# Softplus as one ScalarE function, five of sixteen B products on GpSimd, loops written out: a linear-attention and selective-scan kernel

## The reference

```python
xz = x @ W_in
xh, z = jnp.split(xz, 2, axis=-1)
xh = jax.nn.silu(_causal_conv_k2(xh, conv_w, conv_b))
x_dbl = xh @ W_x
dt_low = x_dbl[..., :DT_RANK]
Bmat = x_dbl[..., DT_RANK:DT_RANK + D_STATE]
Cmat = x_dbl[..., DT_RANK + D_STATE:]
dt = jax.nn.softplus(dt_low @ W_dt + b_dt)
A = -jnp.exp(A_log)
# for every pixel t:  h = exp(dt_t*A)*h + dt_t*B_t*x_t ;  y_t = sum over the states of h*C_t
y = _selective_scan(xh, dt, Bmat, Cmat, A, D)      # + xc * D
y = y * jax.nn.silu(z)
return y @ W_out
```

## Time and profile before

| what | value |
|---|---|
| median of 3 runs | 17306.35 us (17305.44 to 17314.31) |
| the profiled execution's own time | 17308.57 us |
| its span, first to last instruction | 17306.8 us, 188395 instructions |
| PE | 14501.2 us busy (84%) |
| DVE | 14618.9 us busy (84%) |
| ACT | 10286.0 us busy (59%) |
| POOL | 13647.4 us busy (79%) |
| mean granted TensorE clock | 0.886 |

### The profile page before, as it was taken

One profiled execution on the slowest core, in us unless ns is written; L12 is line 12 of the kernel. 1 busy time (PEld: TensorE's weight loads), 2 busy tenths in 40 slices (PEclk: granted clock), 3 DMA queues, 4 the chain that ended last, 5 costly groups with the idle time before them and its releaser, 6 DMA issues. The chain is left out here.

```text
span 17306.8 us, 188395 instructions
## 1 busy us (share of the span) xinstructions
PE 14501.2 (84%) x40250; PEld 5566.1 (32%) x40250; DVE 14618.9 (84%) x14056; ACT 10286.0 (59%) x14202; POOL 13647.4 (79%) x5903
## 2 busy tenths in 40 slices
PE   8999978888888888888888888888888888888876
PEld 3444433333333333333333333333333333333322
DVE  1222239999999999999999999999999999999942
ACT  2222236666666666666666666666666666666642
POOL 0000019999999999999999999999999999999930
PEclk9999988888888888888888888888888888888865
DMA  1111114444444444444444444444444444444445
GB/s 52 38 41 40 43 42 159 159 160 161 161 162 160 157 159 159 160 162 160 162 160 160 156 159 160 162 160 162 160 160 156 159 160 162 160 162 160 160 186 209
DMA packets 508191, 2499.22 MB, mean 144 GB/s; under 512 B 53097, under 2 KB 164938, under 8 KB 226651
## 3 DMA queue, kind: packets, MB, share of 16 engines
q1 hardware_dynamic: 489723, 2419.71, 37.7%
q10 hardware_dynamic: 18208, 76.11, 1.2%
HBM read 2325.05 MB, written 170.57 MB: 144 GB/s over the span
## 5 line engine op out<-in xcount | busy, mean ns | idle before, releaser
L734 POOL TENSOR_TENSOR hc<-h,c_all 128x1024 f32<-128x1024 f32 x4096 | 9526.1, 2354 | 287.9 <-PE y_ps L975 283.2
L975 PE MATMUL y_ps<-hc,ident 128*128 128x512 f32 x16392 | 8032.1, 635 | 900.2 <-POOL hc L734 899.5
L850 ACT ACTIVATE d_a<-dt,a_neg 128x512 f32<-128x512 f32 x8194 | 5596.4, 688 | 4243.9 <-DVE h L1079 4195.4
L1079 DVE TENSOR_TENSOR_SCAN h<-d_a,h,dbx_v 128x512 f32<-128x512 f32 x4960 | 6087.2, 1264 | 25.1
L975 PEld LDWEIGHTS y_ps<-hc,ident 128*128 128x128 f32 x16392 | 3185.3, 203 | 5870.4 <-issue 3862.9
L723 POOL TENSOR_TENSOR dbx_p<-dtx,b_all 128x1024 f32<-128x1024 f32 x1536 | 3613.9, 2353 | 168.4 <-DVE h L1079 168.1
L1079 DVE TENSOR_TENSOR_SCAN h<-d_a,h,dbx_p 128x512 f32<-128x512 f32 x2976 | 3654.0, 1262 | 42.2 <-ACT d_a L850 36.3
L1066 DVE TENSOR_TENSOR dbx_v<-dtx_ps,b_all 128x1024 f32<-128x1024 f32 x2560 | 3013.3, 1201 | 12.9 <-issue 9.3
L479 POOL MEMSET ident_f<- 128x128 f32 x1 | 0.2, 204 | 2438.4 <-POOLq L44 2438.4
L272 PE MATMUL conv_ps<-image,w_taps 128*32 128x512 f32 x11520 | 1785.0, 595 | 0.0
L984 PE MATMUL p_ps<-y,w_out 128*128 128x512 f32 x1028 | 889.8, 1017 | 1020.7 <-DVE dt L1106 1019.4
(11 more groups left out here) (129 smaller groups left out, 10823.4 us busy)
## 6 DMA issues: line engine op xcount, KB each, us to landing
b_all<-bc_dram SPq DMA_DIRECT2D x1028, 1024.0 KB, 6.9
c_all<-bc_dram SPq DMA_DIRECT2D x1025, 1024.0 KB, 4.7
o_dram<-o_sb SPq DMA_DIRECT2D x257, 256.0 KB, 7.4
o_t<-o_dram SPq DMA_DIRECT2D x64, 1024.0 KB, 9.6
out<-r_t ACTq DMA_DIRECT2D x64, 1024.0 KB, 9.2
image<-in_x SPq DMA_DIRECT2D x91, 512.0 KB, 4.1
un<-un_dram SPq DMA_DIRECT2D x516, 34.0 KB
bc_dram<-low_bc SPq DMA_DIRECT2D x257, 64.0 KB, 4.6
```

The lines of the kernel that those rows point to most:

```text
L734: nc.gpsimd.tensor_tensor(hc[:, n % HC], h[:, n], c_all[:, n // CG % 2, n % CG].unsqueeze(1).broadcast_to([128, 2, CH]), ALU.mult).then_in ...
L850: nc.scalar.activation(d_a[:, half], dt[:, p, half], ACT.Exp, scale=a_neg[:, half, n:n + 1]).then_inc(a_done, 1)
L975: last = nc.tensor.matmul(y_ps[:, half], ident[:], hc[:, n % HC, half], start=False, stop=(n == S - 1))
L1079: nc.vector.tensor_tensor_scan(h[:, n, half], d_a[:, half], dbx, zero_col[:] if first else h[:, n, half, CH - 1:CH], ALU.mult, ALU.add).th ...
```

## The change

Softplus becomes a single function of ScalarE, applied once to each half, with the bias inside, from PSUM straight into `dt`. It is in neither of the two table sets in use, and a load of the exp set is written behind it. The three VectorE steps go. `ON_POOL` loses state 14, so VectorE makes 11 products with B and GpSimd 5. The orders in `body` are rearranged: `silu_x` goes from behind decay 4 to behind decay 2, `gate` from behind scan 4 to behind scan 2, `make_dtx` to behind the last GpSimd product, `project_x` behind `add_state` 2, `project_dt` behind `add_state` 5, `copy_out` and `copy_dtx` are moved. Every loop of all stages is written out.

```diff
-            with eng.Fori(0, B) as b:
+            for b in range(0, B):
                 body(b, b * NCH, b * (NCH // 2), 0, 0, True, False)
-                with eng.Fori(0, NCH // 2 - 1) as j:
+                for j in range(0, NCH // 2 - 1):
...
-ON_POOL = [7, 9, 11, 13, 14, 15]
+ON_POOL = [7, 9, 11, 13, 15]
...
             def body(b, km, kh, c, p, first, last):
                 PARITY[0] = p
-                weigh(km, 7)
                 weigh_out(km, 0)
                 weigh_out(km, 1)
+                weigh_out(km, 2)
+                weigh(km, 7)
                 weigh(km, 9)
-                weigh_out(km, 2)
                 weigh_out(km, 3)
                 weigh_out(km, 4)
-                weigh(km, 11)
                 weigh_out(km, 5)
                 weigh_out(km, 6)
+                weigh(km, 11)
                 weigh_out(km, 7)
+                weigh_out(km, 8)
                 weigh(km, 13)
-                weigh_out(km, 8)
-                weigh(km, 14)
-                make_dtx(km, 1 - p)
-                weigh(km, 15)
                 weigh_out(km, 9)
                 weigh_out(km, 10)
                 weigh_out(km, 11)
+                weigh(km, 15)
+                make_dtx(km, 1 - p)
                 weigh_out(km, 12)
...
+            def softplus(km, p):
+
+                after(act, "a_done", 2 * S * km)
+                after(act, "dtx_done", km)
+                for half in range(2):
+                    after(act, f"dt_mm{half}", km + 2)
+                    last = nc.scalar.activation(dt[:, p, half], p_ps[:, half], ACT.Softplus, bias=b_dt[:, half:half + 1])
+                last.then_inc(dt_done, 1)
+                nc.scalar.preload_act_table_set("natural_log_exp_and_others")
...
                 decay(km, 2, 1, p)
+                silu_x(km, q)
+                nc.scalar.preload_act_table_set("natural_log_exp_and_others")
                 decay(km, 3, 0, p)
...
-                silu_x(km, q)
                 decay(km, 5, 0, p)
                 decay(km, 5, 1, p)
                 silu_z(km, q)
                 decay(km, 6, 0, p)
                 decay(km, 6, 1, p)
+                low(km)
                 decay(km, 7, 0, p)
                 decay(km, 7, 1, p)
-                low(km)
                 decay(km, 8, 0, p)
+                decay(km, 8, 1, p)
                 rows(km)
-                decay(km, 8, 1, p)
...
-                biased(km, 0)
                 decay(km, 10, 0, p)
-                biased(km, 1)
-                absolute(km)
                 decay(km, 10, 1, p)
-                exponential(km)
+                softplus(km, q)
                 decay(km, 11, 0, p)
-                plus_one(km)
                 decay(km, 11, 1, p)
-                logarithm(km)
                 decay(km, 12, 0, p)
                 decay(km, 12, 1, p)
+                copy_out(km)
...
                 decay(km, 15, 1, p)
+                copy_dtx(km, q)
...
                 run_scan(km, 1, 0, first)
+                run_scan(km, 1, 1, first)
                 weigh(km, 2)
-                run_scan(km, 1, 1, first)
+                weigh(km, 3)
                 run_scan(km, 2, 0, first)
-                weigh(km, 3)
                 run_scan(km, 2, 1, first)
+                gate(km, q)
+                weigh(km, 4)
                 run_scan(km, 3, 0, first)
                 run_scan(km, 3, 1, first)
-                weigh(km, 4)
-                weigh(km, 5)
                 run_scan(km, 4, 0, first)
                 run_scan(km, 4, 1, first)
-                gate(km, q)
+                weigh(km, 5)
+                weigh(km, 6)
                 run_scan(km, 5, 0, first)
                 run_scan(km, 5, 1, first)
-                weigh(km, 6)
                 weigh(km, 8)
...
                 run_scan(km, 9, 0, first)
+                run_scan(km, 9, 1, first)
                 weigh(km, 10)
-                run_scan(km, 9, 1, first)
                 run_scan(km, 10, 0, first)
+                run_scan(km, 10, 1, first)
                 weigh(km, 12)
-                run_scan(km, 10, 1, first)
-                positive(km)
+                weigh(km, 14)
                 run_scan(km, 11, 0, first)
                 run_scan(km, 11, 1, first)
-                rounding(km)
                 run_scan(km, 12, 0, first)
-                make_dt(km, q)
```

More of the change, by code:

```diff
@@ L163, in _ @@
                 if b + 1 < B:
-                    with sp.Fori(0, PIECES - 3) as j:
+                    for j in range(0, PIECES - 3):
                         sp.wait_ge(conv_done, b * NCH + 2 * j + 7)
@@ L231, in query @@
                 act.dma_start(uq[M:KU, bass.ds(c0, CH)], s_sb[:, p]).then_inc(u_stored[p], 16)
-            with act.Fori(0, B) as b:
-                with act.Fori(0, NCH // 2) as j:
+            for b in range(0, B):
+                for j in range(0, NCH // 2):
                     for p in range(2):
@@ L296, in outer @@
                     last.then_inc(mat_mm, 1)
-            with pe.Fori(0, B) as b:
+            for b in range(0, B):
                 loaded(pe, b)
@@ L412, in _ @@
                         next(between)(b - 1)
-                with dve.Fori(3, NCH // 2 - 1) as j:
+                for j in range(3, NCH // 2 - 1):
                     for i in range(2):
@@ L684, in body @@
                 sp.dma_start(o_dram[:, bass.ds(km * CH, CH)], o_sb[:]).then_inc(o_stored, 16)
-            with sp.Fori(0, B) as b:
+            for b in range(0, B):
                 at = b * (SLOTS * CH) + CH
                 body(b, b * NCH, at + 2 * CH, 0, False)
-                with sp.Fori(0, NCH // 2 - 2) as j:
+                for j in range(0, NCH // 2 - 2):
                     for i in range(2):
@@ L1012, in body @@
                 add_state(km, 2)
-                project_dt(km, 0)
-                project_dt(km, 1)
+                project_x(km, q)
                 add_state(km, 3)
@@ L1017, in body @@
                 add_state(km, 5)
+                project_dt(km, 0)
+                project_dt(km, 1)
                 add_state(km, 6)
@@ L1167, in body @@
                 run_scan(km, 14, 0, first)
+                run_scan(km, 14, 1, first)
                 statistics(b, km, NCH - 1 if first else c - 1)
@@ L1170, in body @@
                     aggregate(b, km)
-                run_scan(km, 14, 1, first)
                 run_scan(km, 15, 0, first)
                 run_scan(km, 15, 1, first)
-            positive(-1)
-            rounding(-1)
-            make_dt(-1, 0)
             chunks(dve, body)
@@ L1233, in _ @@
                 sp.sem_inc(stored[p], 16)
-            with sp.Fori(0, B) as b:
-                with sp.Fori(0, NCB // 2) as j:
+            for b in range(0, B):
+                for j in range(0, NCB // 2):
                     for p in range(2):
@@ L1247, in _ @@
             nc.scalar.activation(g_std[:], g_m2[:], ACT.Sqrt, bias=eps[:]).then_inc(rooted, 1)
-            with act.Fori(0, B) as b:
+            for b in range(0, B):
                 act.wait_ge(ab_done, 2 * b + 2)
-                with act.Fori(0, NCB // 2) as j:
+                for j in range(0, NCB // 2):
                     for p in range(2):
@@ L1268, in _ @@
             pe.wait_ge(step, STEPS_BEFORE_ROOT)
-            with pe.Fori(0, B) as b:
-                with pe.Fori(0, NCB // 2) as j:
+            for b in range(0, B):
+                for j in range(0, NCB // 2):
                     for p in range(2):
@@ L1310, in _ @@
             dve.sem_inc(added, 2)
-            with dve.Fori(0, B) as b:
+            for b in range(0, B):
                 dve.wait_ge(silu_done, b * NCB + 2)
@@ L1318, in _ @@
                                       ).then_inc(gm_done, 1)
-                with dve.Fori(0, NCB // 2) as j:
+                for j in range(0, NCB // 2):
                     for p in range(2):
```

63 lines of the change are left out of this document (6 added, 57 removed).

## The result

| | before | after |
|---|---|---|
| median of four runs | 17307.02 us (17305.44 to 17314.31) | 16723.14 us (16713.74 to 16726.66) |
| the profiled execution's span | 17306.8 us | 16712.0 us |

The ratio of the times is 0.9661, with a 95% interval of 0.9644 to 0.9678: the changed kernel is 583.9 us faster, where 574 were predicted. The time of 16732 us was 9 us too high.

What follows compares the result with a forecast made beforehand. VectorE was taken to bound the scan stage, 81% of the time. 256 x (2.24 - 0.05) = 561 us, with 5 and 8 outside it 574 us less, gave 16732 us; range 16590 to 16930.

Steps and rivals of the forecast that it cites:

- the main term: VectorE in each chunk: three softplus operations go and one product with B comes, 2.24 us less.
- The new wait: VectorE's gate, moved earlier, waits for states 12 to 15: 0 to 1.3 us a chunk, 0.45 on average.
- The old waits: VectorE's existing waits of 0.43 us a chunk, hanging on ScalarE steps gone or moved: 0.40 goes.
- ScalarE's covers: VectorE's work while a ScalarE block runs: `silu_x` fits by 1.6 us, `silu_z` and Softplus by 0.5 each.
- GpSimd stays second: GpSimd's 22 products take 50.8 us a chunk, 1.7 below VectorE's 52.5; second only with waits under 1.7.
- An image's last chunk: Gate and `inner` wait for `w_xz`: about 7 us, eight times, 6 us more, set against the loop jumps' gain.
- Outside the scan stage: Ahead of the first chunk 5 us less, first stage 8 us less (0 to 10), last stage unchanged.
- No wait at all at the gate: Rival: TensorE's clock recovers in time and old waits go too, 0.45 us less a chunk, 16610 us; chance 0.15.
- The missed cover: Rival: a ScalarE block overruns its 0.5 us spare, twice a chunk, 1 us more, 16990 us; chance 0.17.
- A drain at the switch: Rival: the new table's switch costs a drain, Softplus block 2.8 us longer, 17320 us, no change; chance 0.03.
- TensorE at the low clock up to the gate: Rival: states 12 to 15 wholly at 1.2 GHz, chunk 5.2 us longer than now, 18600 us; chance 0.04.
- late code: Rival: never-repeated code comes late, waits of 1.5 us twice a chunk on VectorE or ScalarE, 17460 us; chance 0.02.

Runs made afterwards that it cites:

- the kernel with the filler: The changed kernel with eight idle matmuls of 128x256 in TensorE's pause behind `add_state` 11: 16627.97 us, ratio 0.9607 to the kernel before.
- Softplus alone: Against the kernel before with all loops written out: Softplus as one function behind decay 10, old order, six products on GpSimd; 16963.48 us, ratio 0.9802 to the kernel before.

## Why the prediction was right

- **The bound and the main term.** VectorE set the end before and after, and two operations less at a pitch of 1.12 us are 2.24 us a chunk. The measured difference of the periods is 2.20, with 2.19 forecast.
- **The new wait, 0.45 us forecast.** Inside the images it measured 0.38 us a chunk; the 0.44 of the stretch has the images' ends in it, for which the prediction had a term of its own. The cause is the one named: state 12 was ready 0.5 us into the chunk (0.3 forecast) and the pause ahead of it was 4.93 us (5). The kernels with idle matmuls show it. Two sizes were off and made up for each other. The room was 1.2 us and not 1.7, since the sum let the five groups run in a row, while state 13 comes 2.31 us behind state 12. The loss was 1.1 or 2.3 us in the two chunks shown and not evenly spread between 1.3 and 3. That the average came out so near is luck; the range of 0 to 1.3 was the honest statement.
- **The old waits, 0.40 us forecast to go.** VectorE's idle time without the gate's was 90.4 us in the stretch 2700 to 16000 before, 0.37 a chunk, 74.8 with the loops written out, and 46.5 after, 0.18. So only 0.19 went, and 0.06 of that was the loops', whose gain I had put at the images' ends only. This term was twice too large.
- **ScalarE's covers.** 0.65 us was taken for a Softplus, 0.68 measured. Both covers tested, 0.5 and 1.6 us of spare, held against a load of 1.28: the one broke and the other did not. The cover of `silu_z` was not tested.
- **GpSimd.** 1 to 2 us of waiting in front of `weigh` 11, for the slot of scan 7, forecast; 1.7 measured, but in front of `weigh_out` 6, for scan 6 itself. By the prediction's own sum that step was ready at 26.7 us and scan 6 done at 26.6, so the two places were within 0.1 us, and it looked at one only. That GpSimd stays second was right, but with less room than "1.7 below" says: its 50.8 us of work and 1.7 of waiting fill the period of 52.71. The run with six products shows what one more brings.
- **An image's last chunk.** Waits at the gate of about 7 us were forecast there, eight times; they are 1.5 to 3.7, 2.1 on average. The step that `w_xz` would come as late against the gate as before was wrong, by some 5 us eight times, 0.15 us a chunk in the kernel's favour. This about makes up for the old waits that stayed: the total is right in part because two terms were off in opposite ways.
- **Outside the scan stage.** 13 us forecast, 31 in the profiled run. The mis-sized term is the first stage: with the loops alone it gave 22.6, where 8 was taken out of a bound of 0 to 10. The bound came from seven jumps of at most 1.5 us, ScalarE's in the earlier trace rows, put at the images' ends alone. There the gain was 12 us, 1.7 each, a little over the bound; and 11 us more came within the images, which the bound left out. The prologue gave some 7 us where 5 was forecast.
- **The rivals.** No wait at all at the gate, 16610 (16617 by its own terms): this is the kernel with the filler, 16628; it took other means. The missed cover, 16990, did not happen; the load added behind Softplus shows how it would have begun. A drain at the switch, TensorE at the low clock up to the gate, and late code (17500 and not 17460 by its own terms) did not occur: the loads stand 10 ns from their neighbours, the clock was back at 1.00 some 5 to 8 us behind the pause, and straight code was faster.

Two sizes were missed behind the prediction, in experiments that each undid one step: putting a product back on GpSimd (1.86 us a chunk where 0.6 was expected) and moving the gate by one scan (1.93 where a gain was expected). The gate's move cost four times the wait that it was to mend. That the two come to nearly the same is explained by no run.

What stays open: the loops' share within the changed kernel was not measured, only that in the kernel before; and what the product moved to VectorE would bring in the old order.

## What to carry to other kernels

Where two engines are busy for 97% and 99%, work taken from one counts only up to the other: Softplus alone brought a third of what it took off VectorE, and 240 us more came only with the new order and the one product that changed sides together; the order by itself made the kernel slower. Add an engine's waits for the bound engine to its own work before calling it second. And look at what an engine does in its pauses: a pause that costs nothing by itself can halve TensorE's clock for the work behind it, and a few idle matmuls gave back 0.57% of the whole kernel.

## What the hardware showed that was not expected

- A pause of TensorE of 2.9 us had the low clock behind it (four records at 3.78 us and not 1.98, in the kernel with the gate moved), while one of 1.49 us behind idle matmuls left it at 1.00. Behind pauses of 3.2 us, with four idle matmuls, the next eight records took 4.3, 5.4 or 6.6 us, and the gain was about 40% of that with eight.
- The ends of the hardware loops cost 22.6 us in the first stage, 1.7 us at each change of image on TensorE among them, and 28.8 us, 0.11 a chunk, in the scan stage, where every engine had a jump at every second chunk.
- A table load of an unused set costs 0, 0.5 or 0.9 us of the period for the same 1.28 us, by where it stands and what else waits.
